# Low weight parts of one expert on GpSimd, one rounding moved, the weight loads written out: a cross-attention and mixture-of-experts kernel on one core

## The chip, the cores and the metric

The kernel runs on one core of one Trainium2 chip. The metric is the device time of one execution in microseconds (us). The engines that matter are TensorE (PE; its weight loads are listed as PEld), VectorE (DVE), ScalarE (ACT), GpSimd (POOL) and SyncE (SP), which issues the large loads and stores. The engines run their own instruction lists in order and meet only at semaphores.

## The reference, cut to what matters

```python
x = x + xattn(ctx, ctx, layernorm(x))            # a long convolution per head, 32 heads
h = layernorm(x)                                 # 2048 tokens of 512
scores = softmax(h @ gate_w.T)                   # 16 experts, the best 4 of each token
...
xg  = xpad[buf]                                  # up to 256 tokens gathered per expert
mid = silu(xg @ w_gate[e]) * (xg @ w_up[e])      # 512 -> 352
y  += scatter(mid @ w_down[e] * wbuf[e])         # 352 -> 512
x  = x + y + shared_ffn(h)
```

Every matrix product of the expert part is done in three passes on numbers split in a high part (rounded to fp32r) and a low part (what is left): high by high, high by low, low by high. So each weight block and each gathered row block needs a rounding (the high part, on ScalarE) and a subtraction (the low part, on VectorE) before TensorE can use it. The tokens are 2048 rows of 512 numbers; `CAP` is 256 and there are 16 experts.

## The kernel before, in words

The first part (to about 345 us) works on head groups: convolutions of key and value products on TensorE, products and sums on VectorE, the pair products and low parts on GpSimd, and the router and the shared feed-forward layer of the group before in between. The second part is a pipeline over the 16 experts. The order of each engine is written out by hand in a function `unit(e, k, ...)` per engine; `k` is `e % 2` and picks one of two sets of buffers. What `unit(e)` holds:

- TensorE: `expert_gu(e, k, 0)` and `expert_gu(e, k, 1)` (24 matmuls each; gate and up products of 128 of the 352 columns), `slots(e + 2)` (16 small matmuls that find the rows of expert e + 2), `rows_t(e + 1)` (8 transposes of the gathered rows of the next expert into PSUM), `expert_down(e - 1)` (18 matmuls) and `expert_gu(e, k, 2)`. The first `expert_gu` of an expert waits for all of its high weights (`ew_h`), all of its low weights (`ew_l`), and the high and low rows (`g_h`, `g_l`).
- ScalarE: four `split_w(e + 1, ., c)` (L1105, the high weights of chunk c, 128 x 704), `e_silu` and `e_round` of each of the three middles (L1134, L1140), `round_rows(e + 1)` (L1127, the high rows, two instructions), `split_d(e)` (L1110, L1111) and `weigh(e - 1)`.
- VectorE: `one_hot(e + 2)` (L1763, 128 x 2048 bf16), `low_w(e + 1, ., c)` for c = 0 to 3 (L1786, 128 x 704 each), `e_middle` and `e_low` of each middle (L1802, L1809), `decode(e + 2)` (five small instructions, L1769 to L1780, that give the row numbers for the gather), `low_rows(e + 1)` (L1794, two instructions) and `low_d(e)` (L1815, L1817). The order is one_hot, low_w 0, low_w 1, e_middle 0, low_w 2, e_low 0, decode, e_middle 1, low_rows, low_w 3, e_low 1, low_d.
- GpSimd: `gather(e + 2)` (L1377, two indirect DMAs) once `decode` has signalled `sl_ok`, and `scatter(e - 1)` (L1390). Between them it has nothing to do.
- SyncE: `next_raw(e)` waits until the high and low parts of the weights of expert e are made, loads the weights of expert e + 2 into the same buffer (L488, L489), waits for the high and low down weights of expert e and loads those of e + 2 (L492, L494). It stood in a hardware loop over pairs of experts.

`unit(0)` is special on every engine: there is no expert before it (`before` is False), so `e_middle(-1, 2)`, `e_low(-1, 2)`, `expert_down(-1)` and `weigh(-1)` are missing, and the weights of expert 1, loaded late because their buffer was in use by the shared layer, are split in it.

Of the kernel before, what the change touches and what calls it, by code (L numbers as in the profile page):

```python
# [18 lines left out]
fp32 = mybir.dt.float32  # L19
# [3 lines left out]
ALU = mybir.AluOpType  # L23
# [7 lines left out]
def wait(eng, sem, value):  # L31

    if not (isinstance(value, int) and value <= 0):
        eng.wait_ge(sem, value)


def xattn_moe_kernel(nc, x, ctx, taps, skip, gate_w, w_gate, w_up, w_down, sw_gate, sw_up, sw_down, out):
    B, ROWS, L = x.shape
    H = taps.shape[0]
    HD = ROWS // H  # L40
    E, _, I = w_gate.shape
    IS = sw_gate.shape[1]
    CAP, TOPK, EPS = 256, 4, 1e-5
    T = B * ROWS
    LB = L // P
# [37 lines left out]
    with es:  # L83
        def sem(name):
            return es.enter_context(nc.semaphore(name))
# [7 lines left out]
        def place(name, shape, dt):  # L93
            size = 1
            for n in shape[1:]:
                size *= n
            size = -(-size * (2 if dt == bf16 else 4) // 32) * 32
            t = nc.alloc_sbuf_tensor_at(name, shape, dt, offset=cursor[0])
            cursor[0] += size
            assert cursor[0] <= arena_base + arena_bytes, (name, cursor[0])  # L100
            return t
# [137 lines left out]
        raw_w = [raw_w0, place("raw_w1", [P, LB, 2 * I], fp32)]  # L239
        raw_d = [raw_d0, place("raw_d1", [P, EJ, L], fp32)]  # L240
        ew = [ew0, place("ew1", [P, LB, 2, 2 * I], fp32r)]
# [55 lines left out]
        rt_c = sem("rt_c")  # L297
        rt_go, rt_step, rt_w = sem("rt_go"), sem("rt_step"), sem("rt_w")
        ew_h, ew_l, ed_h, ed_l = sem("ew_h"), sem("ew_l"), sem("ed_h"), sem("ed_l")
        vals_ok = sem("vals_ok")  # L300
        oh_ok, sl_mm, sl_ok, sl_cp = sem("oh_ok"), sem("sl_mm"), sem("sl_ok"), sem("sl_cp")
        chain = sem("chain")
# [62 lines left out]
        def _(sp):  # L365
# [121 lines left out]
            def load_raw_w(e, k):  # L487
                sp.dma_start(raw_w[k][:, :, 0:I], wg_e[e]).then_inc(raw_in[k], 16)  # L488
                sp.dma_start(raw_w[k][:, :, I:2 * I], wu_e[e]).then_inc(raw_in[k], 16)  # L489

            def load_raw_d(e, k):
                sp.dma_start(raw_d[k][:, 0:2, :], w_down[e, 0:2 * P, :].rearrange("(j p) l -> p j l", p=P))\  # L492
                    .then_inc(rawd_in[k], 16)
                sp.dma_start(raw_d[k][0:EK[2], 2, :], w_down[e, 2 * P:I, :]).then_inc(rawd_in[k], 16)  # L494
# [13 lines left out]

            def next_raw(e, k):
                sp.wait_ge(ew_h, LB * (e + 1))  # L510
                sp.wait_ge(ew_l, LB * (e + 1))
                load_raw_w(e + 2, k)
                sp.wait_ge(ed_h, e + 1)
                sp.wait_ge(ed_l, e + 1)
                load_raw_d(e + 2, k)

            with sp.Fori(0, E // 2 - 1) as i:
                for k in range(2):
                    next_raw(2 * i + k, k)
            sp.wait_ge(out_out, 16 * TT * NG)  # L520
            sp.wait_ge(xn_out, 16 * TT * NG)
            sp.wait_ge(added, 16 * HALVES * E)
# [3 lines left out]
        def _(pe):  # L526
# [289 lines left out]
            def expert_gu(e, k, j):  # L816
                m = EK[j]
                if j == 0:
                    pe.wait_ge(ew_h, LB * e + LB)
                    pe.wait_ge(ew_l, LB * e + LB)  # L820
                    pe.wait_ge(g_h, HALVES * e + HALVES)
                    pe.wait_ge(g_l, HALVES * e + HALVES)
                if isinstance(e, int) and e == 0 and j == TT:
                    pe.wait_ge(mid_ok, SJ * (NG - 1) + 4)
                wait(pe, e_mid, EJ * e - EJ + j + 1)
                for u in range(2):
                    for c in range(LB):
                        for a, b in PASSES:
                            col = u * I + j * P
                            last = pe.matmul(egu[j][0:m, u * CAP:(u + 1) * CAP], ew[k][:, c, a, col:col + m],  # L830
                                             xgT[k][:, c, b, :], start=(c == 0 and (a, b) == PASSES[0]),
                                             stop=(c == LB - 1 and (a, b) == PASSES[-1]))
                last.then_inc(e_mm, 1)
# [75 lines left out]
        def _(act):  # L909
# [192 lines left out]
            def split_w(e, k, c):  # L1102
                act.wait_ge(raw_in[k], 32 * ((e - k) // 2) + 32 if isinstance(e, int) else e * 16 + (32 - 16 * k))
                wait(act, e_mm, EJ * e - EJ)
                act.activation(ew[k][:, c, 0, :], raw_w[k][:, c, :], ACT.Copy).then_inc(ew_h, 1)  # L1105

            def split_d(e, k):
                act.wait_ge(rawd_in[k], 32 * ((e - k) // 2) + 32 if isinstance(e, int) else e * 16 + (32 - 16 * k))
                wait(act, e_dn, HALVES * e - HALVES)
                act.activation(ed[k][:, 0:2, 0, :], raw_d[k][:, 0:2, :], ACT.Copy)  # L1110
                act.activation(ed[k][0:EK[2], 2, 0, :], raw_d[k][0:EK[2], 2, :], ACT.Copy).then_inc(ed_h, 1)  # L1111
# [11 lines left out]
            def round_rows(e, k):  # L1123
                for h in range(HALVES):
                    act.wait_ge(g_tr, HALVES * e + h + 1)
                    wait(act, e_mm, EJ * e - EJ)
                    act.activation(xgT[k][:, :, 0, h * P:(h + 1) * P],  # L1127
                                   yb[:, h, :].rearrange("p (c n) -> p c n", c=LB), ACT.Copy).then_inc(g_h, 1)
# [7 lines left out]
            def e_round(e, k, j):  # L1136
                m, s = EK[j], (EJ * k + j) % 2
                act.wait_ge(e_mid, EJ * e + j + 1)
                wait(act, e_dn, HALVES * e - HALVES)
                act.activation(midh[0:m, EJ * k + j, :], mid[0:m, s, :], ACT.Copy).then_inc(e_midh, 1)  # L1140

            def unit(e, k, before):
                if before:
                    e_round(e - 1, 1 - k, 2)
                for c in range(LB):
                    split_w(e + 1, 1 - k, c)
                e_silu(e, k, 0)
                e_round(e, k, 0)
                e_silu(e, k, 1)
                e_round(e, k, 1)  # L1150
                round_rows(e + 1, 1 - k)
                split_d(e, k)
                if before:
                    weigh(e - 1, 1 - k)
                e_silu(e, k, 2)
# [24 lines left out]
            for e in range(1, E - 2):  # L1180
                unit(e, e % 2, True)
            unit(E - 2, 0, True)
            last_unit(E - 1, 1)


        @block.gpsimd
        def _(pool):
# [183 lines left out]
            def gather(e, k):  # L1371
                pool.wait_ge(sl_ok, e + 1)
                wait(pool, g_tr, HALVES * e - HALVES)
                wait(pool, carried[0], e)
                pool.memset(carrier[:, 0:1], 0.0).then_inc(carried[0], 1)  # L1375
                for h in range(HALVES):
                    pool.indirect_dma_start(xg[k][:, h, :], None, xn_dram,  # L1377
                                            bass.IndirectOffsetOnAxis(slot_rows[:, e, h:h + 1], 0),
                                            bounds_check=T - 1, oob_is_err=False).then_inc(rows_in[k], 16)
# [14 lines left out]
            def unit(e, k, before, next2):  # L1394
                if next2:
                    gather(e + 2, k)
                if before:
                    scatter(e - 1, 1 - k)
# [10 lines left out]
            pool.wait_ge(xn_out, 16 * TT * NG)  # L1409
            gather(0, 0)  # L1410
            gather(1, 1)
            unit(0, 0, False, True)
            for e in range(1, E - 2):
                unit(e, e % 2, True, True)
# [6 lines left out]
        def _(dve):  # L1421
# [361 lines left out]
            def low_w(e, k, c):  # L1783
                dve.wait_ge(ew_h, LB * e + c + 1)
                wait(dve, e_mm, EJ * e - EJ)
                dve.tensor_tensor(ew[k][:, c, 1, :], raw_w[k][:, c, :], ew[k][:, c, 0, :].bitcast(fp32),  # L1786
                                  ALU.subtract).then_inc(ew_l, 1)
# [32 lines left out]
            def unit(e, k, before, next2):  # L1820
                if before:
                    e_middle(e - 1, 1 - k, 2)
                if next2:
                    one_hot(e + 2)
                if before:
                    e_low(e - 1, 1 - k, 2)
                low_w(e + 1, 1 - k, 0)
                low_w(e + 1, 1 - k, 1)
                e_middle(e, k, 0)
                low_w(e + 1, 1 - k, 2)  # L1830
                e_low(e, k, 0)
                if next2:
                    decode(e + 2, k)
                e_middle(e, k, 1)
                low_rows(e + 1, 1 - k)
                low_w(e + 1, 1 - k, 3)
                e_low(e, k, 1)
                low_d(e, k)
                if e and 2 * e + 2 < E:
                    values(2 * e + 2, 2 * e + 4)  # L1840
# [80 lines left out]
```

## Time and profile before

| | us |
|---|---|
| time, median of 3 runs (lowest, highest) | 617.8 (617.42, 619.48) |
| the profiled execution's own time | 618.2 |
| its span, first to last instruction | 616.2 |
| PE, busy of the span | 586.8 (95%) |
| DVE, busy | 486.3 (79%) |
| POOL, busy | 389.9 (63%) |
| ACT, busy | 291.5 (47%) |
| mean granted clock of TensorE, share of full speed (1.00 in every slice after 100 us but the last) | 0.989 |
| TensorE idle in the span's rest after 392 us, for other engines | 1.8, in one wait |

How to read it: the profiled execution is one execution, and its span leaves out 2.0 us (618.2 less 616.2) before the first and after the last instruction. From about 392.4 us to 600 us TensorE works without a gap, with a period of 14.03 us for an expert; the experts' part begins for TensorE at 380.65 us with `expert_gu(0, 0, 0)`. Where a row says "<-DVE ew L1786", the instruction's wait ended when that VectorE instruction signalled.

### The profile page before, as it was taken

The numbers are of one execution on the slowest core, as the hardware profiler recorded it, in microseconds if no ns is written. First come the engines' busy times: TensorE is split into PE (matmuls) and PEld (weight loads), VectorE is DVE, ScalarE is ACT, GpSimd is POOL, SyncE is SP. The second block draws the span as 40 slices with busy tenths as digits, with TensorE's granted clock in tenths as the row PEclk, the third lists the DMA queues.
The fourth block names the chain that finished last, engine by engine and source line by source line (L and its number), as shares of the span: only waits on it lengthen the run. The fifth ranks groups of instructions, "written<-read, shape, count | busy, mean of one in ns | idle before, by whom it ended". The sixth has DMA issues, their size and how long they took to land.

```text
span 616.2 us, 13661 instructions
## 1 busy us (share of the span) xinstructions
PE 586.8 (95%) x4387; PEld 550.3 (89%) x4387; DVE 486.3 (79%) x1279; ACT 291.5 (47%) x521; POOL 389.9 (63%) x502
## 2 busy tenths in 40 slices
PE   3969999999999999999999999899999999999993
PEld 3759998999999999989999898899999999999992
DVE  6998787679779779599699879989887888887730
ACT  2525334434434435345262334566655666656731
POOL 6998898878888888789771282178344433334342
PEclk9988999999999999999999999999999999999997
DMA  6475215136325336142240146788878888788443
GB/s 192 181 250 169 74 70 167 49 86 179 82 80 153 81 94 170 43 132 64 82 115 2 51 160 229 236 245 223 233 222 216 228 233 244 234 230 247 128 55 47
DMA packets 60489, 92.01 MB, mean 149 GB/s; under 512 B 4260, under 2 KB 36004, under 8 KB 60440
## 3 DMA queue, kind: packets, MB, share of 16 engines
q1 hardware_dynamic: 53168, 74.53, 39.3%
q0 software_dynamic: 7168, 16.78, 13.1%
q8 instruction: 27, 0.44, 0.3%
q14 instruction: 22, 0.18, 0.1%
q10 hardware_dynamic: 104, 0.08, 0.0%
HBM read 74.29 MB, written 17.08 MB: 148 GB/s over the span
## 4 chain that ended last, share of the span: by engine, by line
PE 79%; DVE 10%; issue 3%; POOL 3%; ACT 2%; DMA 1%; DVEq 1%; POOLq 0%; SPq 0%; ACTq 0%
PE gu L678 18%; PE gu L830 14%; PE yb L558 11%; PE mb L847 10%; PE gu L716 7%; PE yb L830 7%; PE yb L608 4%; PE mb L530 4%; PE yb L530 2%; DVE prod L1494 2%; DVE oT L1512 1%; POOL kv L1233 1%; DVE prod L1496 1%; DVE ew L1786 1%; PE yb L801 1%
## 5 line engine op out<-in xcount | busy, mean ns | idle before, releaser
L678 PE MATMUL gu<-xT,sw 128*128 128x256 f32 (+2 forms) x1104 | 136.3, 281 | 0.0
L678 PEld LDWEIGHTS gu<-xT,sw 128*128 128x128 f32 (+2 forms) x1104 | 131.8, 180 | 0.4 <-issue 0.2
L1233 POOL TENSOR_TENSOR kv<-kT 128x256 f32 (+3 forms) x232 | 106.8, 499 | 0.0
L1250 POOL TENSOR_TENSOR kvl<-kv,kvh 128x1440 fp32r<-128x1440 f32 (+1 forms) x28 | 87.7, 3131 | 25.7 <-ACT kvh L957 25.5
L1494 DVE TENSOR_TENSOR prod<-yb,qT 128x64 f32<-128x64 f32 (+10 forms) x272 | 74.5, 284 | 18.8 <-PE yb L608 13.5
L957 ACT ACTIVATE kvh<-kv 128x1440 fp32r<-128x1440 f32 (+1 forms) x28 | 37.5, 1339 | 76.1 <-POOL kv L1240 36.9
L1512 DVE TENSOR_REDUCE oT<-prod 128x256 f32<-128x2048 f32 x32 | 72.9, 2277 | 0.1
L558 PE MATMUL yb<-kvh,tlast 128*128 128x288 f32 x280 | 66.1, 297 | 0.0
L1496 DVE TENSOR_TENSOR prod<-yb,qT 128x96 f32<-128x96 f32 (+10 forms) x238 | 63.9, 268 | 0.0
L847 PE MATMUL mb<-ed,midh 128*128 128x512 f32 x180 | 57.4, 400 | 0.0
L1786 DVE TENSOR_TENSOR ew<-raw_w,ew 128x704 fp32r<-128x704 f32 x64 | 55.1, 881 | 0.3 <-ACT ew L1105 0.3
L1375 POOL MEMSET carrier<- 128x1 f32 x16 | 2.5, 158 | 80.8 <-DVE slot_rows L1780 80.8
L830 PE MATMUL gu<-xgT,ew 128*128 128x256 f32 x384 | 47.2, 282 | 1.8 <-DVE ew L1786 1.8
L830 PEld LDWEIGHTS gu<-xgT,ew 128*128 128x128 f32 x384 | 46.4, 190 | 2.1 <-issue 2.0
L558 PEld LDWEIGHTS yb<-kvh,tlast 128*128 128x128 f32 x280 | 48.1, 188 | 0.0
L1105 ACT ACTIVATE ew<-raw_w 128x704 fp32r<-128x704 f32 x64 | 45.4, 777 | 4.5 <-DMA raw_w<-in_L_ffn_w_up_dram 4.5
L830 PE MATMUL gu<-xT,ew 128*128 128x256 f32 x384 | 47.0, 282 | 0.0
L830 PEld LDWEIGHTS gu<-xT,ew 128*128 128x128 f32 x384 | 46.3, 190 | 0.1
L1258 POOL TENSOR_TENSOR midl<-mid,midh 128x256 fp32r<-128x256 f32 x36 | 26.3, 737 | 28.6 <-ACT midh L983 28.5
L1140 ACT ACTIVATE midh<-mid 128x256 fp32r<-128x256 f32 (+1 forms) x48 | 20.1, 418 | 49.6 <-DVE mid L1802 49.6
L716 PE MATMUL gu<-sd,midh 128*128 128x512 f32 x140 | 43.5, 392 | 0.0
L1377 POOL DMA_INDIRECT xg<-normalised_tokens,slot_rows x32 | 33.6, 1051 | 15.1 <-issue 15.1
(219 smaller groups left out, 1322.3 us busy)
## 6 DMA issues: line engine op xcount, KB each, us to landing
raw_w<-in_L_ffn_w_gate_dram SPq DMA_DIRECT2D x16, 704.0 KB, 7.8
raw_w<-in_L_ffn_w_up_dram SPq DMA_DIRECT2D x16, 704.0 KB, 9.2
raw_d<-in_L_ffn_w_down_dram SPq DMA_DIRECT2D x16, 512.0 KB, 4.3
tlast<-toeplitz_taps SPq DMA_DIRECT2D x20, 384.0 KB, 3.6
tstep<-tap_steps SPq DMA_DIRECT2D x20, 256.0 KB, 4.1
c_t<-in_ctx_dram SPq DMA_DIRECT2D x16, 256.0 KB, 4.8
x_t<-in_x_dram SPq DMA_DIRECT2D x16, 256.0 KB, 5.0
toep<-toeplitz_taps SPq DMA_DIRECT2D x8, 512.0 KB, 3.8
```

The source lines that it names most:

```text
L558: last = pe.matmul(yb[:, lb, 0:PW], taps_of(a), (kvh, kvl)[b][:, s, m, :], start=(i == 0 and (a, b) == PASSES[0]), stop=(i == len(parts) - ...
L678: last = pe.matmul(bank[0:m, u * GT:(u + 1) * GT], sw[:, c, a, col:col + m], xT[:, c, b, :], start=(c == 0 and (a, b) == PASSES[0]), stop= ...
L716: last = pe.matmul(sums[:, t, :], (midh, midl)[a][:, j, cols], sd[:, j, b, :], start=False, stop=(j == SJ - 2 and (a, b) == PASSES[-1]))
L830: last = pe.matmul(egu[j][0:m, u * CAP:(u + 1) * CAP], ew[k][:, c, a, col:col + m], xgT[k][:, c, b, :], start=(c == 0 and (a, b) == PASSES ...
L847: last = pe.matmul(mb[:, h, :], lhs[0:EK[j], EJ * k + j, h * P:(h + 1) * P], ed[k][0:EK[j], j, b, :], start=(j == 0 and (a, b) == PASSES[0 ...
L1105: act.activation(ew[k][:, c, 0, :], raw_w[k][:, c, :], ACT.Copy).then_inc(ew_h, 1)
L1233: last = pool.tensor_tensor(to[:, :, POFF[d]:POFF[d] + w], src[:, :, 0:w], src[:, :, d * B:HD * B], ALU.mult)
L1250: pool.tensor_tensor(kvl[:, s, 0:nb, :], kv[:, s, 0:nb, :], kvh[:, s, 0:nb, :].bitcast(fp32), ALU.subtract)\
L1494: last = dve.tensor_tensor(prod[:, lo:hi, d * B // 2:HD * B // 2, d, :], pair, first, ALU.mult)
L1496: last = dve.tensor_tensor(prod[:, lo:hi, 0:w // 2, HD - d, :], pair, second, ALU.mult)
L1512: dve.tensor_reduce(oT[:, :, hl * HD * B:(hl + 1) * HD * B].rearrange("p c (a u) -> p c a u", u=2), prod[:].rearrange("p c a i u -> p c a ...
L1786: dve.tensor_tensor(ew[k][:, c, 1, :], raw_w[k][:, c, :], ew[k][:, c, 0, :].bitcast(fp32), ALU.subtract).then_inc(ew_l, 1)
```

## The change

Three edits, all at the start of the expert pipeline or in who signals whom:

1. The low weight parts of expert 1 for chunks 2 and 3 are computed by GpSimd, right after it has issued the gathers of experts 0 and 1, and no longer by VectorE in `unit(0)`. They signal a new semaphore `ew_lp`; the consumers of low weights (TensorE, and SyncE before it loads over them) wait for both from expert 1 on.
2. In ScalarE's `unit(0)` the rounding of the second middle, `e_round(0, 0, 1)`, comes behind `round_rows(1)` in place of ahead of it.
3. SyncE's loop of weight loads is written out, 14 times `next_raw`.

```diff
+        ew_lp = sem("ew_lp")
+        LENT = LB // 2
+
+        def low_weights(eng, e):
+            first = isinstance(e, int) and e == 0
+            eng.wait_ge(ew_l, LB * e + (LB if first else LB - LENT))
+            if not first:
+                eng.wait_ge(ew_lp, LENT)
...
             def next_raw(e, k):
                 sp.wait_ge(ew_h, LB * (e + 1))
-                sp.wait_ge(ew_l, LB * (e + 1))
+                low_weights(sp, e)
                 load_raw_w(e + 2, k)
...
-            with sp.Fori(0, E // 2 - 1) as i:
-                for k in range(2):
-                    next_raw(2 * i + k, k)
+            for e in range(E - 2):
+                next_raw(e, e % 2)
...
                 if j == 0:
                     pe.wait_ge(ew_h, LB * e + LB)
-                    pe.wait_ge(ew_l, LB * e + LB)
+                    low_weights(pe, e)
...
                 e_silu(e, k, 1)
-                e_round(e, k, 1)
+                if before:
+                    e_round(e, k, 1)
                 round_rows(e + 1, 1 - k)
+                if not before:
+                    e_round(e, k, 1)
                 split_d(e, k)
...
             gather(0, 0)
             gather(1, 1)
+            for c in range(LB - LENT, LB):
+                pool.wait_ge(ew_h, LB + c + 1)
+                pool.tensor_tensor(ew[1][:, c, 1, :], raw_w[1][:, c, :], ew[1][:, c, 0, :].bitcast(fp32),
+                                   ALU.subtract).then_inc(ew_lp, 1)
             unit(0, 0, False, True)
...
                 low_w(e + 1, 1 - k, 1)
                 e_middle(e, k, 0)
-                low_w(e + 1, 1 - k, 2)
+                if before:
+                    low_w(e + 1, 1 - k, 2)
                 e_low(e, k, 0)
                 if next2:
                     decode(e + 2, k)
                 e_middle(e, k, 1)
                 low_rows(e + 1, 1 - k)
-                low_w(e + 1, 1 - k, 3)
+                if before:
+                    low_w(e + 1, 1 - k, 3)
                 e_low(e, k, 1)
```

## Rows read from the trace of the kernel before

**Rows 1.** Timeline of TensorE: start, length, line, what, how many, idle before it.

```profile
387.60 3.06 PE L830 MATMUL yb<-xT,ew 128*96 128x256 f32 x24
392.43 5.95 PE L830 MATMUL gu<-xgT,ew 128*128 128x256 f32 x48 [1.78 <-DVE ew L1786]
```

**Rows 2.** The chain that ended last, in order of time: start, length, what.

```profile
403.89 2.84 PE yb L830 x24
406.72 5.71 PE gu L830 x48
```

**Rows 3.** Timeline of VectorE in unit(0): start, length, line, what.

```profile
382.91 2.28 DVE L1763 TENSOR_TENSOR onehot<-iota_c,rank_in 128x2048 bf16<-128x2048 bf16 x1
385.11 1.69 DVE L1786 TENSOR_TENSOR ew<-raw_w,ew 128x704 fp32r<-128x704 f32 x2
386.71 0.41 DVE L1802 TENSOR_TENSOR mid<-sil,gu 128x256 f32<-128x256 f32 x1
387.04 0.89 DVE L1786 TENSOR_TENSOR ew<-raw_w,ew 128x704 fp32r<-128x704 f32 x1
387.84 0.42 DVE L1809 TENSOR_TENSOR midl<-mid,midh 128x256 fp32r<-128x256 f32 x1
...
388.85 0.42 DVE L1802 TENSOR_TENSOR mid<-sil,gu 128x256 f32<-128x256 f32 x1
390.24 1.29 DVE L1794 TENSOR_TENSOR xgT<-yb,xgT 128x512 fp32r<-128x512 f32 x2 [0.97 <-ACT xgT L1127]
391.45 0.88 DVE L1786 TENSOR_TENSOR ew<-raw_w,ew 128x704 fp32r<-128x704 f32 x1
```

**Rows 4.** Timeline of ScalarE in unit(0).

```profile
381.44 2.84 ACT L1105 ACTIVATE ew<-raw_w 128x704 fp32r<-128x704 f32 x4 [1.98 <-DMA raw_w<-in_L_ffn_w_up_dram]
...
387.16 0.42 ACT L1140 ACTIVATE midh<-mid 128x256 fp32r<-128x256 f32 x1 [2.61 <-DVE mid L1802]
387.48 0.36 ACT L1134 ACTIVATE sil<-gu 128x256 f32<-128x256 f32 x1
389.31 0.42 ACT L1140 ACTIVATE midh<-mid 128x256 fp32r<-128x256 f32 x1 [1.46 <-DVE mid L1802]
389.63 1.06 ACT L1127 ACTIVATE xgT<-yb 128x512 fp32r<-128x512 f32 x2
```

**Rows 5.** Line L1273, GpSimd's low parts of shared weights: ns min/median/max, starts.

```profile
L1273 POOL TENSOR_TENSOR sw<-sw_raw,sw x6: 1668/1692/1719, 30.9 to 49.7; 128x704 fp32r<-128x704 f32 x6
```

**Rows 6.** Timeline of both engines, 83.36 to 84.91 us, one instruction a row.

```profile
83.36 0.69 DVE L1440 TENSOR_TENSOR sd<-x,sd 128x512 fp32r<-128x512 f32 x1
83.44 0.93 POOL L1233 TENSOR_TENSOR kv<-kT 128x128 f32<-128x128 f32 x1
83.96 0.95 DVE L1440 TENSOR_TENSOR sd<-x,sd 128x512 fp32r<-128x512 f32 x1
```

**Rows 7.** Groups by shape, 8 to 20 us: a GpSimd 128-wide product, mean ns.

```profile
L1233 POOL TENSOR_TENSOR kv_more<-kT 128x128 f32<-128x128 f32 x1 | 0.5, 451 | 0.0
```

**Rows 8.** Timeline at 362 to 365 us, both engines.

```profile
362.21 2.29 DVE L1763 TENSOR_TENSOR onehot<-iota_c,rank_in 128x2048 bf16<-128x2048 bf16 x1
362.62 2.17 POOL L1365 TENSOR_TENSOR wt<-wrest,V 128x64 f32<-128x64 f32 x1
```

**Rows 9.** Timeline at 200 to 203 us, both engines.

```profile
200.17 3.31 POOL L1250 TENSOR_TENSOR kvl<-kv,kvh 128x1440 fp32r<-128x1440 f32 x1 [0.55 <-ACT kvh L957]
202.75 0.41 DVE L1548 TENSOR_TENSOR mid<-sil,gu 128x256 f32<-128x256 f32 x1
```

**Rows 10.** Timeline of GpSimd: the last indirect DMA of expert 2's gather.

```profile
391.04 1.00 POOL L1377 DMA_INDIRECT xg<-normalised_tokens,slot_rows  x1 [0.30 <-issue]
```

**Rows 11.** Line L1377 as a whole: from issue to landing.

```profile
DMA to landing us min/median/max: 3.3/3.6/5.4
```

**Rows 12.** Waits of SyncE's queue, 380 to 600 us: total us, times, longest.

```profile
SPq L514 <- DVE ed L1817: 150.7, 14, 11.8
```

**Rows 13.** Timeline of TensorE's weight loads at 603 us.

```profile
603.45 0.30 PEld L858 LDWEIGHTS mb<-ed,midh 96*128 96x128 f32 x2 [0.24 <-issue]
```

## The prediction

> **What bounds the kernel now.** I read the page first. Its busy shares name TensorE (586.8 of 616.2 us), and its chain of waits ends in the experts' part almost wholly in TensorE lines. Then I asked where TensorE is idle there. The chain in order of time shows no gap inside the pipeline: the 24 matmuls at 403.89 us take 2.84, and the next group starts at 406.72, where they end [rows 2]. The timeline of TensorE has one hole: `expert_gu(0, 0, 2)` starts at 387.60, and the next group, `expert_gu(1, 1, 0)`, only at 392.43, after 1.78 us of idle that a VectorE instruction of L1786 ended [rows 1]. A stream of 24 such matmuls takes 2.84, so TensorE could have gone on at 387.60 + 2.84 = 390.44, and the whole hole is 392.43 - 390.44 = 1.99 us. Behind it TensorE is full, so whatever moves the start of `expert_gu(1, 1, 0)` moves the end of the kernel by the same amount, and nothing else in this change can move it by more than that hole on the good side.
>
> The timeline of VectorE then tells what fills the time up to 392.43 [rows 3]: one_hot from 382.91, low_w 0 and 1 of expert 1 from 385.11, the first middle at 386.71, low_w 2 at 387.04, e_low at 387.84, decode, the second middle at 388.85, 0.97 idle, low_rows from 390.24, low_w 3 from 391.45 to 392.33. The idle 0.97 is ScalarE's: it rounds the second middle at 389.31 and only then the rows at 389.63 [rows 4].
>
> **What the change takes out, if nothing gets in its way.** Three terms, each read between starts in [rows 3]:
> - low_w 2 goes. From the start of the first middle to that of e_low it was 387.84 - 386.71 = 1.13. Now e_low waits for ScalarE's rounding, which starts 0.04 behind the middle's end and takes 0.42 [rows 4]: 0.41 + 0.04 + 0.42 and 0.04 to signal are 0.91. Gain 0.22.
> - The rows are rounded ahead of the second middle, so low_rows can follow that middle at once: 390.24 - 388.85 = 1.39 becomes 0.33, the spacing of such a middle (387.04 - 386.71). Gain 1.06.
> - low_w 3 goes: 392.33 less the end of low_rows at 391.53. Gain 0.80.
>
> These are 2.08 us, and low_rows would end at 391.53 - 1.28 = 390.25. With 0.10 us to signal (392.33 to 392.43) TensorE could start at 390.35, before it has finished its own work at 390.44. So undisturbed the hole is gone, and the gain is 1.99.
>
> **What it adds.** Two subtractions of 128 x 704 on GpSimd. The same form on the same engine is on record at L1273, where nothing disturbs it: 1.69 us [rows 5]. They can start when ScalarE has made the high parts of chunks 2 and 3: four in 2.84 us from 381.44, so chunk 2 at about 383.6 and chunk 3 at 384.3 [rows 4]; GpSimd has issued its two gathers by then. Alone they would be over at 387.0, three microseconds ahead of need.
>
> But they are not alone. VectorE and GpSimd hold each other up in this trace whenever both read two operands from SBUF. At 83.36 VectorE starts a subtraction of that kind (0.69). GpSimd's 128-wide product, issued at 83.44, takes 0.93 [rows 6] where 0.45 is its length undisturbed [rows 7]: it ends at 84.37, 0.32 after VectorE's end. VectorE's next subtraction, issued at 83.96, takes 0.95 in place of 0.69 and ends at 84.91, 0.54 behind GpSimd's. So they take turns, one whole instruction each, also where VectorE has its next one ready, and a handed-over turn costs the instruction's own length less 0.13 (GpSimd, 0.45 - 0.32) or 0.15 (VectorE, 0.69 - 0.54). One_hot holds GpSimd up too: a 64-wide GpSimd instruction issued at 362.62 under a one_hot that ran to 364.50 took 2.17 and ended at 364.79 [rows 8]. A VectorE instruction that reads PSUM, such as a middle, isn't held up: 0.41 in the midst of a GpSimd subtraction of 3.31 [rows 9].
>
> Now the order of VectorE in unit(0) has one_hot, low_w 0 and low_w 1 back to back, all three with both operands in SBUF, exactly where GpSimd becomes ready. Step by step:
> - GpSimd's chunk 2 is issued at 383.65 under one_hot, which ends at 385.19 [rows 3]. It gets the turn: 385.19 + 1.69 - 0.13 = 386.75.
> - VectorE's low_w 0, issued at 385.11, waits for it: 386.75 + 0.88 - 0.15 = 387.48.
> - GpSimd's chunk 3 had queued up behind low_w 0: 387.48 + 1.56 = 389.04.
> - low_w 1 waits for that: 389.04 + 0.73 = 389.77.
> - The first middle starts 0.08 before that end, at 389.69. It was 386.71, so it is 2.98 late.
>
> All that follows on VectorE up to low_rows shifts with it. The sum for the start of `expert_gu(1, 1, 0)`: + 2.98 - 0.22 - 1.06 - 0.80 = + 0.90 us. Checked forward: middle 389.69, e_low 390.60, second middle 1.01 later (388.85 - 387.84) at 391.61, low_rows 391.94 to 393.23, TensorE 393.33, against 392.43. ScalarE is in time for it: round 390.14 to 390.56, the silu that follows to 390.84, the rows in 1.06 to 391.9, just ahead of low_rows.
>
> The Trainium skill, in SBUF — State Buffer (section "Who interferes with whom"), gives the reason in general terms: a VectorE instruction with two SBUF inputs takes its second one through the read port that GpSimd uses, and whichever comes second blocks fully. By that rule the sum is the + 0.90 above; without it the sum would be the gain of 1.99. The trace agrees with it by the 2.17 and the 0.95.
>
> **What follows behind it.** The gather of expert 2 waits for `decode`, which is 2.76 late (391.61 for 388.85): its last indirect DMA starts at 391.04 + 2.76 = 393.80 [rows 10] and, with the longest landing on record, 5.4 [rows 11], has landed by 399.2. TensorE asks for those rows 6.11 after the start of `expert_gu(1, 1, 0)` with 48 matmuls and the slots (5.71 + 0.40), so at 399.4. That is covered, by 2.0 at the median landing of 3.6. One_hot of expert 3 and e_low of the third middle come 1.4 later (low_d then waits for ScalarE's split of the down weights, which the moved rounding puts behind the rows) and are still over before TensorE reaches them. VectorE has slack in each unit (79% busy), so the rest catches up. SyncE's loads of expert 3 wait for low_d, as they always do (14 waits, the longest 11.8) [rows 12], about 1.4 later than before; the weights are needed a whole unit after.
>
> **The small edits.** The written-out loop takes two register moves out of an iteration of a queue that is idle for 150 us [rows 12]: 0, with a rival below. The second wait of TensorE, once for each of 15 experts, stands behind four others that cost no gap today [rows 2]: 0 from below; the one place where TensorE's queue takes time for waits in sight is 0.24 us at 603.45 [rows 13], an upper end of 15 x 0.24 = 3.6. I take 0, the row nearest to it being the very place.
>
> **The sum.** The profiled execution took 618.2 us; + 0.9 is 619.1. It lay 0.4 above the median of the runs, 617.8, so the median after should be 618.7.
>
> **Rivals.**
> - *No hold-up* (the two engines don't disturb each other in these instructions): the hole closes, - 1.99, so 615.8. For it speaks only that a VectorE instruction with one operand in PSUM runs undisturbed [rows 9], which these are not; against it [rows 6, 8].
> - *VectorE keeps its turn* while it has instructions ready. Then one_hot and both low_w run as before to 386.80, GpSimd's chunk 2 comes under the first middle (386.80 + 1.56 = 388.36), e_low ends at 388.36 + 0.27 = 388.63, chunk 3 at 390.19, and the small instruction of `decode` that reads two SBUF operands waits for that. The second middle starts at about 390.5, low_rows ends at 392.1, TensorE starts at 392.2: - 0.2, so 617.6. Against it: VectorE's two subtractions at 83.36 and 83.96 let one of GpSimd in between [rows 6].
> - *TensorE's added wait shows* (slower): at each of the 15 places where the wait for `ew_lp` stands, the weight loads start late because the queue has one more instruction to work off than the running matmuls cover. From 0.07 a place on (0.07 x 15 = 1.05, with 0.9 past 0.3%) it decides; at the 0.24 of [rows 13] it is 3.6 + 0.9 = 4.5, so 622.3. Against it: four waits cost nothing there now.
> - *The written-out loads come late* in steady state, by fetches of instructions that a loop doesn't need. It would take over 3 us a load before ScalarE waits; then every expert is late. I give it almost nothing.
>
> **How the numbers follow.** The turn-taking case 0.60; VectorE keeps its turn 0.12; no hold-up 0.13; the added wait 0.07; anything else, such as a gather that lands late, 0.08. A difference of 0.3% (1.85 us, that is 615.95 or 619.65) is about what can be told from no change here. The first case has its own range of 617.9 to 619.9: a turn may cost 0.2 more or less, and the median of three runs moves by half a microsecond (the three lie 2.06 apart). Of it 0.10 lies past 619.65. No hold-up lies at 615.8, just past the lower bound; I count all of it as faster, with 0.03 of the rest. So faster 0.16, slower 0.10 + 0.07 + 0.03 = 0.20, the same 0.64. The range runs from 615.7, which takes in the closed hole, to 620.5, which leaves out most of the added wait.
>
> **What would show it.** Right: in unit(0) GpSimd's first subtraction takes about 3.1 us (383.65 to 386.75) and the second about 2.3; low_w 0 takes 2.4 and low_w 1 2.3 in place of 0.88; TensorE's hole before `expert_gu(1, 1, 0)` is 2.7 in place of 1.78, ended by low_rows (L1794), not by L1786; behind it the period stays 14.03. Wrong: low_w at 0.88 and GpSimd's at 1.69 would mean no hold-up; a hole under 1.78 with both GpSimd instructions behind low_w 1 would mean the other order; gaps of a tenth at the start of every expert would be the added wait.

## The result and the profile after

The changed kernel took 620.69 us (median of 9 runs, 619.22 to 622.04), the kernel before 617.99 (9 runs, 617.42 to 619.56): ratio 1.0035, 95% interval 1.0026 to 1.0044. It is slower by about 2.2 us by the ratio and 2.7 by the medians. The forecast was 618.7, 0.9 slower, in a range of 615.7 to 620.5; the median lies 0.2 past that range, while 2.2 on top of the 617.8 that the forecast started from is 620.0, within it. Line numbers of the changed kernel are higher: VectorE's low_w is L1800, low_rows L1808, GpSimd's new line L1424, `expert_gu` L837.

The timeline of TensorE, changed kernel (start, length, what, idle before it), answers to [rows 1]:

```profile
387.95 3.06 PE L837 MATMUL yb<-xT,ew 128*96 128x256 f32 x24
393.83 7.45 PE L837 MATMUL gu<-xgT,ew 128*128 128x256 f32 x48 [2.83 <-DVE xgT L1808]
```

Two things are to be seen. The hole (the idle time of TensorE ahead of these 48 matmuls) is 2.83 us in place of 1.78, and low_rows ends it. And the 48 matmuls behind it take 7.45 in place of 5.95. The timelines of VectorE and GpSimd, each instruction by itself, answer to [rows 3]:

```profile
383.25 2.28 DVE L1777 TENSOR_TENSOR onehot<-iota_c,rank_in 128x2048 bf16<-128x2048 bf16 x1
383.85 3.23 POOL L1424 TENSOR_TENSOR ew<-raw_w,ew 128x704 fp32r<-128x704 f32 x1 [1.13 <-ACT ew L1112]
385.44 2.38 DVE L1800 TENSOR_TENSOR ew<-raw_w,ew 128x704 fp32r<-128x704 f32 x1
387.04 2.34 POOL L1424 TENSOR_TENSOR ew<-raw_w,ew 128x704 fp32r<-128x704 f32 x1
387.75 2.38 DVE L1800 TENSOR_TENSOR ew<-raw_w,ew 128x704 fp32r<-128x704 f32 x1
390.06 0.41 DVE L1816 TENSOR_TENSOR mid<-sil,gu 128x256 f32<-128x256 f32 x1
392.30 1.28 DVE L1808 TENSOR_TENSOR xgT<-yb,xgT 128x512 fp32r<-128x512 f32 x2
```

GpSimd waits for the end of one_hot, VectorE for GpSimd, GpSimd for VectorE, VectorE for GpSimd: one instruction each. 3.23, 2.38, 2.34, 2.38 where 3.1, 2.4, 2.3, 2.3 were forecast. The busy time by stage shows the rest. Each row has the stage and its length, the busy time of PE, PEld, DVE, ACT and POOL with counts, then the granted clock of TensorE as a share of full speed, the DMA share and GB/s. Changed kernel:

```profile
393.83:401.28 7.45, 7.45 (x54) 7.40 (x55) 7.03 (x10) 4.44 (x9) 1.03 (x2) 0.77 0.76 223
409.63:423.66 14.03, 14.03 (x116) 13.19 (x116) 12.41 (x26) 8.66 (x16) 5.57 (x7) 1.00 0.89 233
...
394.00:395.00 1.00, 1.00 (x6) 1.00 (x6) 0.67 (x1) 0.56 (x2) 0.83 (x1) 0.51 0.44 90
395.00:396.00 1.00, 1.00 (x7) 1.00 (x6) 1.00 (x2) 0.00 (x0) 0.16 (x1) 0.50 0.68 201
397.00:398.00 1.00, 1.00 (x8) 1.00 (x8) 1.00 (x1) 1.00 (x2) 0.00 (x0) 0.78 0.62 86
398.00:399.00 1.00, 1.00 (x11) 1.00 (x10) 1.00 (x3) 1.00 (x3) 0.00 (x0) 1.00 0.91 305
```

The same stretch before:

```profile
392.43:398.38 5.95, 5.95 (x54) 5.90 (x55) 5.95 (x8) 3.41 (x6) 0.00 (x0) 1.00 0.61 182
```

Behind the hole the granted clock is 0.50 (1.2 of 2.4 GHz) from 394.0 to 397.4 us, then full again; later experts keep their 14.03. The difference of the two profiled executions, 616.2 to 618.9, adds up so: `expert_gu(0, 0, 0)` starts 0.32 later (380.97 for 380.65; this comes from ahead of the change, where one wait of TensorE near 8 us took 4.75 for 3.73); from `expert_gu(0, 0, 2)` to `expert_gu(1, 1, 0)` it is 5.88 for 4.83, so 1.05 more; the matmuls at half clock 1.50 more; the rest gives back 0.17.

### The profile page after: what moved, and what is told of

Its sections match the earlier page's. It is cut to its first block, busy times and chain, and to the rows that moved or that the text cites. A ratio compares the mean times of both kernels' runs of the same rounds, so it can differ in the third digit from the quotient of the medians.

```text
span 618.9 us, 13563 instructions
## 1 busy us (share of the span) xinstructions
PE 587.3 (95%) x4387; PEld 550.9 (89%) x4387; DVE 487.3 (79%) x1277; ACT 291.4 (47%) x521; POOL 383.4 (62%) x504
## 4 chain that ended last, share of the span: by engine, by line
PE 79%; DVE 10%; issue 3%; POOL 3%; ACT 2%; DMA 1%; DVEq 1%; POOLq 0%; SPq 0%; ACTq 0%
PE gu L685 18%; PE gu L837 14%; PE yb L565 11%; PE mb L854 10%; PE gu L723 7%; PE yb L837 6%; PE yb L615 4%; PE mb L537 4%; PE yb L537 2%; DVE prod L1508 2%; DVE oT L1526 1%; POOL kv L1243 1%; DVE prod L1510 1%; DVE ew L1800 1%; PE yb L808 1%
## 5 line engine op out<-in xcount | busy, mean ns | idle before, releaser
L1800 DVE TENSOR_TENSOR ew<-raw_w,ew 128x704 fp32r<-128x704 f32 x62 | 56.5, 931 | 0.3 <-ACT ew L1112 0.3
L837 PE MATMUL gu<-xgT,ew 128*128 128x256 f32 x384 | 48.7, 287 | 2.8 <-DVE xgT L1808 2.8
L837 PEld LDWEIGHTS gu<-xgT,ew 128*128 128x128 f32 x384 | 47.9, 195 | 3.1 <-issue 3.0
L837 PE MATMUL gu<-xT,ew 128*128 128x256 f32 x384 | 47.0, 282 | 0.0
L837 PEld LDWEIGHTS gu<-xT,ew 128*128 128x128 f32 x384 | 46.4, 190 | 0.1
```

## The experiments

Ratios are to the kernel before, run beside each group on the same chip: its median was 618.32 for `e1` to `e4`, 617.63 for `e5` to `e8` and 618.38 for `e9`.

**Who holds VectorE up: GpSimd's reads.** `e1_no_read`

```diff
-                pool.tensor_tensor(ew[1][:, c, 1, :], raw_w[1][:, c, :], ew[1][:, c, 0, :].bitcast(fp32),
-                                   ALU.subtract).then_inc(ew_lp, 1)
+                pool.memset(ew[1][:, c, 1, :].bitcast(fp32), 0.0).then_inc(ew_lp, 1)
```

> The changed kernel, in which GpSimd fills the two low chunks of expert 1 with zeros (it writes the same places and signals the same, but reads nothing from SBUF; the low parts of these two chunks are left out of the products). Taking turns over reads of SBUF (my theory): low_w 0 and 1 of VectorE are back at 0.88 each (1.69 for both, where the changed kernel has 4.69), the hole of TensorE ahead of expert 1 closes (under 0.2 us idle, where the changed kernel has 2.83), no clock is lost, and the time is 2.0 below before, 0.9968 of it. If GpSimd's writes, or its work as such, hold VectorE up (rival): low_w keeps over 2 us each and the hole stays over 1.5. If the written-out loads or the added waits cost (rival): the hole closes, but the time stays within 0.5 of before or above it.

Ratio 0.9963 (0.9950 to 0.9977), 616.03 us. TensorE waits for no engine there, the 48 matmuls start at 390.70 with 5.93. VectorE and GpSimd side by side:

```profile
383.10 2.28 DVE L1776 TENSOR_TENSOR onehot<-iota_c,rank_in 128x2048 bf16<-128x2048 bf16 x1
385.30 1.69 DVE L1799 TENSOR_TENSOR ew<-raw_w,ew 128x704 fp32r<-128x704 f32 x2
383.80 1.37 POOL L1424 MEMSET ew<- 128x704 f32 x2 [1.23 <-ACT ew L1112]
```

GpSimd's two writes (383.80 to 385.17) lie wholly under one_hot, which keeps its 2.28. So writing the same places costs nothing; it is the instructions that read that take turns. The same run has the written-out loads and the added waits in it, and they don't keep it from its gain.

**The moved rounding alone.** `e2_round_only`: the kernel before with the change's second edit.

> The kernel before with the second edit alone: the second middle of expert 0 is rounded behind the rows of expert 1. By the terms of the prediction low_rows comes 1.06 earlier, low_w 3 still follows it, the hole shrinks from 1.78 to about 0.7, and the time is 1.06 below before: ratio 0.9983. Rival, that the rounding was covered by something else that is late (the rows from PE, or the silu ahead of it): the hole stays at 1.5 or more and the ratio at 1.000.

Ratio 0.9982 (0.9971 to 0.9992), 616.69 us, the hole 0.70. The term of 1.06 is right: 1.78 - 0.70 = 1.08. **The changed kernel without it**, `e5_no_move`:

> The changed kernel without its second edit: the second middle of expert 0 is rounded ahead of the rows again. By the turns and the term of 1.06 for the rounding, low_rows comes 1.06 later than in the changed kernel, TensorE's idle time is 2.83 + 1.06 = 3.9 us, the clock is at half speed behind it in all executions (48 matmuls in 7.4), and the time is 0.90 + 1.06 + 1.5 = 3.5 above before: ratio 1.0055. If the taking of turns already hides the rounding (rival, since ScalarE is idle longer there): the idle time stays at 2.8 and the ratio at that of the changed kernel, 1.0035.

Ratio 1.0062 (1.0044 to 1.0079), 622.22 us; the idle time is 3.88, 1.05 more than in the changed kernel:

```profile
393.73 1.29 DVE L1805 TENSOR_TENSOR xgT<-yb,xgT 128x512 fp32r<-128x512 f32 x2 [0.97 <-ACT xgT L1134]
395.27 6.91 PE L837 MATMUL gu<-xgT,ew 128*128 128x256 f32 x44 [3.88 <-DVE xgT L1805]
```

These are VectorE's low_rows and TensorE's group behind the hole (this view ends at 402 us; all 48 matmuls take 7.39); the 0.97 for ScalarE is back. So the second edit shortens the idle time by about 1.05 us with and without the first. With the written-out loads near nothing (`e6` below), the loss comes from the first.

**Whether the idle time lowers the clock.** `e3_hole_one`, and `e4_hole_two` with `range(2)`: the kernel before with extra VectorE work that lengthens the hole, GpSimd not involved.

```diff
                 low_rows(e + 1, 1 - k)
+                if not before:
+                    for i in range(1):
+                        dve.tensor_tensor(ew[1][:, 3, 1, :], raw_w[1][:, 3, :], ew[1][:, 3, 0, :].bitcast(fp32),
+                                          ALU.subtract).then_inc(again, 1)
+                        dve.wait_ge(again, i + 1)
                 low_w(e + 1, 1 - k, 3)
```

> The kernel before with one more subtraction of 128x704 on VectorE ahead of low_w 3 in unit(0), GpSimd not involved: the hole of TensorE grows from 1.78 by about 0.95 to 2.7 us, near the 2.83 of the changed kernel. If the length of TensorE's idle time is what makes the granted clock fall (theory): some or all executions show the clock at 0.5 for about 3 us after the hole, the 48 matmuls take 7.4 in place of 5.95, and the time is 0.95 + 0 to 1.5 above before (ratio 1.0015 to 1.004). If the clock fell for another reason that goes with the change, such as GpSimd and VectorE at work together (rival): 48 matmuls stay at 5.95 and the time is 0.95 above before (1.0015).

> As the one before, with two more subtractions: the hole grows by about 1.9 to 3.7 us. Theory (the idle time makes the clock fall): the clock is at 0.5 for some us behind the hole in all executions, 48 matmuls at 7.4 or more, time 1.9 + 1.5 = 3.4 above before, ratio 1.0055. Rival (another reason): 5.95, time 1.9 above before, ratio 1.003.

With two, ratio 1.0055 (1.0042 to 1.0068), 621.61 us. The hole is 3.31, less than the 3.7 expected. The group behind it:

```profile
394.58 7.29 PE L831 MATMUL gu<-xgT,ew 128*128 128x256 f32 x48 [3.31 <-DVE ew L1787]
```

One microsecond of that group by stage, with its clock of 0.50:

```profile
395.00:396.00 1.00, 1.00 (x6) 1.00 (x6) 1.00 (x2) 0.00 (x0) 0.00 (x0) 0.50 0.00 0
```

The clock falls to 0.50 as in the changed kernel, with nothing of the change in the code. With one, ratio 1.0033 (1.0021 to 1.0045), but the profiled execution shows a hole of 2.71 with the clock full and 5.94 for the 48 matmuls; the other seven executions had spans of 617.4 to 618.9 for its 616.3. The longer hole as profiled is worth 0.93 us, a ratio of 1.0015, which lies below that interval, so most of the others lost more than that. Where they lost it their times don't tell; second profiles of this kernel and of the changed one were to show it:

> The kernel with VectorE's one more subtraction, once more: a second profile. Seven of its eight executions had a span of 617.4 to 618.9, the profiled one 616.3 at full clock behind a hole of 2.71. If the fall of the clock is a matter of chance for a hole of this length (theory), a second profile may show 0.5 for some us behind a hole of the same 2.7, with 48 matmuls in about 7.4. If the others were longer for another reason (rival), the clock is full here too and the extra time lies elsewhere.

> The changed kernel once more: a second profile. The turns are the same to 0.05 us (low_w 0 and 1 in 4.69, GpSimd's two in 5.5, idle 2.8), whatever the clock does behind the hole: 0.5 for about 3 us, 48 matmuls in 7.4 and a span of 618 to 619, or full, 5.95 and a span of 616.4 to 617.4.

`e10_hole_one_again` again showed 2.66 idle, a full clock and a span of 616.3, so what the seven had stays unseen. The changed kernel again (`e11_changed_again`, span 618.7) had 2.73 idle and 7.45 for the matmuls:

```profile
393.24:400.69 7.45, 7.45 (x54) 7.40 (x55) 7.03 (x10) 4.44 (x9) 1.03 (x2) 0.77 0.69 210
```

So in the experts' part the clock held behind 1.75, 1.78, 2.66 and 2.71 us of idle time and fell behind 2.73, 2.83, 3.31 and 3.88 (and 5.8, in `e8` below). The fall doesn't come with TensorE's restart: by stages cut finer it came 0.5 and 0.2 us behind the restart in the two profiles of the changed kernel (393.76 for 393.24, 394.02 for 393.83), and 0.4 and 0.2 ahead of it, with TensorE still idle, in `e4` (394.14 for 394.58) and `e5` (395.08 for 395.27). So 2.7 us isn't shown to be a fixed limit, and no profile shows both outcomes of one kernel; what decides near it stays open. The spread of the spans (one of eight at 616.3 here; two of nine at 616.4 and 617.1 in the changed kernel) fits a fall in some executions and not in others, but proves little: the kernel before, with its hole of 1.78, has spans from 614.9 to 617.6 of its own.

The kernel before has such a pause too, far ahead of the experts. TensorE's timeline, then by stage the first 2.95 us of the pause and the 5.85 us of work behind it, in the kernel before:

```profile
43.73 1.09 PE L530 MATMUL mb<-ident,oT 128*128 128x128 f32 x4 [3.94 <-DVE oT L1512]
```

```profile
39.80:42.75 2.95, 0.00 (x0) 0.00 (x0) 2.92 (x11) 0.78 (x2) 2.95 (x3) 1.00 1.02 266
43.73:49.58 5.85, 5.85 (x25) 5.85 (x26) 3.09 (x10) 2.61 (x4) 4.64 (x5) 0.50 0.36 136
```

Behind 3.94 us of idle time TensorE worked 5.85 us at half clock. So the trace of before already held a sign that a pause can cost more than its length.

**The written-out loads alone.** `e6_written_out`

> The kernel before with the third edit alone, SyncE's loads written out 14 times. Theory: the queue waits for low_d anyway, period of an expert 14.03, ratio 1.000. Rival, late loads by fetches of instructions: ScalarE's split of weights waits for DMA in some expert and the period grows; over 1.001.

Ratio 1.0008 (0.9999 to 1.0018), 618.14 us: no difference that can be told, and the profile shows none, with a span of 615.5 and a hole of 1.75. The interval leaves room for up to 1 us.

**A version meant to beat both.** `e7_chunk_wait`: all low parts on VectorE, the rounding moved, and TensorE waits for the last chunk only where it uses it.

```diff
                 if j == 0:
-                    pe.wait_ge(ew_l, LB * e + LB)
+                    pe.wait_ge(ew_l, LB * e + LB - (1 if e == 1 else 0))
...
                     for c in range(LB):
+                        if e == 1 and j == 0 and u == 0 and c == LB - 1:
+                            pe.wait_ge(ew_l, LB * e + LB)
```

> A version meant to beat both: all on VectorE as before, the second edit (the rounding moved), and TensorE waits for the low part of expert 1's chunk 3 only ahead of the first matmul that needs it, the 10th of the group, 9 x 0.119 = 1.07 us in. low_rows ends at 390.47 in the times of the kernel before, so TensorE starts at 390.57, 1.86 earlier than 392.43; low_w 3 is done at 391.3, ahead of 391.64. Idle under 0.2, no clock lost, ratio 0.9970. If the wait in the middle of the group stops the weight loads that run ahead (rival): a gap of some tenths at the 10th matmul, ratio 0.9975 to 0.998.

Ratio 0.9975 (0.9966 to 0.9985), 616.24 us, faster than both kernels. Most of it is the moved rounding, which alone gave 0.9982 (0.9971 to 0.9992) in `e2`; the intervals overlap, so what the later wait adds is shown by the profiles and not by the times: from `expert_gu(0, 0, 2)` to `expert_gu(1, 1, 0)` it is 3.14 us here (390.37 - 387.23) and 3.76 there. TensorE and VectorE's low_rows in its timeline:

```profile
387.23 3.06 PE L832 MATMUL yb<-xT,ew 128*96 128x256 f32 x24
388.83 1.28 DVE L1799 TENSOR_TENSOR xgT<-yb,xgT 128x512 fp32r<-128x512 f32 x2
390.37 5.95 PE L832 MATMUL gu<-xgT,ew 128*128 128x256 f32 x48
```

The wait in the middle of the group costs nothing (5.95 for the 48 matmuls, as before). The start misses the ideal 387.23 + 2.84 = 390.07 by 0.30: it comes 0.26 after low_rows ends at 390.11. I had put 0.10 on that signal.

**GpSimd beside an instruction that reads PSUM.** `e8_one_beside`: the changed kernel with `LENT = 1`, low_w 2 back on VectorE, and

```diff
                 pool.wait_ge(ew_h, LB + c + 1)
+                pool.wait_ge(e_mid, 2)
                 pool.tensor_tensor(...)
```

> The changed kernel, in which GpSimd does chunk 3 alone, and only once the second middle is there, so that it runs beside VectorE's low_rows, which read PSUM; VectorE keeps low_w 2. Theory (only instructions with both operands in SBUF take turns with it): GpSimd's subtraction takes 1.69, low_rows keep 1.28 for both, e_low behind them waits for GpSimd (0.5 more), and TensorE starts when GpSimd is done, 389.27 + 0.05 + 1.69 + 0.1 = 391.1 in the times of before, 1.3 earlier: ratio 0.998. Rival (any VectorE instruction is held up by a GpSimd one): low_rows end only with GpSimd's, at 391.1 + 1.2 = 392.3, TensorE at 392.4, ratio 1.000.

Ratio 1.0106 (1.0091 to 1.0121), 623.99 us: a miss, though the point in question came out as the theory had it.

```profile
388.56 1.28 DVE L1809 TENSOR_TENSOR xgT<-yb,xgT 128x512 fp32r<-128x512 f32 x2
389.76 1.03 DVE L1824 TENSOR_TENSOR midl<-mid,midh 128x256 fp32r<-128x256 f32 x1
392.79 2.28 DVE L1778 TENSOR_TENSOR onehot<-iota_c,rank_in 128x2048 bf16<-128x2048 bf16 x1
388.79 1.71 POOL L1425 TENSOR_TENSOR ew<-raw_w,ew 128x704 fp32r<-128x704 f32 x1 [7.03 <-DVE mid L1817]
392.00 5.08 POOL L1387 DMA_INDIRECT xg<-normalised_tokens,slot_rows  x1 [0.30 <-issue]
```

VectorE first, then GpSimd: GpSimd's 1.71 and low_rows' 1.28 lie side by side undisturbed; e_low, with both operands in SBUF, waits (1.03 for 0.42). TensorE resumed at 390.70. But the gather of expert 2, now behind GpSimd's subtraction, met one_hot, and its second DMA kept GpSimd for 5.08 us in place of 1.00. The waits of TensorE, and its stage behind that wait:

```profile
PE yb L537 <- DMA xg<-normalised_tokens,slot_rows: 5.8, 1, 5.8
```

```profile
402.82:406.24 3.42, 3.42 (x12) 3.09 (x13) 1.47 (x3) 2.01 (x3) 0.00 (x0) 0.50 0.27 78
```

So the loss is the 5.8 us of waiting and, behind it, 3.4 us of work at half clock, less the 1.2 gained at the hole (3.61 for 4.83 from group to group).

**What held the gather.** `e9_late_hot`: the same with

```diff
+                if isinstance(e, int) and e == 1:
+                    dve.tensor_reduce(carrier_d[:, 0:1], ew[1][:, 0, 0, :].bitcast(fp32), AX.X, ALU.max)
                 if next2:
                     one_hot(e + 2)
```

> The kernel with GpSimd's one chunk beside low_rows, and in VectorE's unit(1) a reduction of 128x704 with one operand in SBUF (about 0.8 us, its result unused) ahead of one_hot of expert 3, so that one_hot and what follows it start after the second indirect DMA of expert 2's gather has been worked off by GpSimd. In the kernel without it that DMA took 5.08 us of GpSimd's time (392.00 to 397.08), and TensorE waited 5.8 us for the rows. Theory (what holds the indirect DMA is VectorE's row of two-operand instructions, one_hot, e_low, low_w 0 and 1, that it runs into): it takes 1.00 again, the rows are there in time, TensorE's wait of 5.8 is gone, and the time is that of a start 1.3 earlier than before, ratio 0.998 (0.997 to 0.999). Rival (it was held by the loads on the DMA engines, or by being issued close behind GpSimd's own subtraction): it stays over 4 us, ratio above 1.008.

Ratio 0.9993 (0.9982 to 1.0004), 617.74 us. VectorE and GpSimd in its timeline:

```profile
392.84 0.87 DVE L1839 TENSOR_REDUCE carrier_d<-ew 128x1 f32<-128x704 f32 x1
393.64 2.27 DVE L1778 TENSOR_TENSOR onehot<-iota_c,rank_in 128x2048 bf16<-128x2048 bf16 x1
392.05 1.41 POOL L1387 DMA_INDIRECT xg<-normalised_tokens,slot_rows  x1 [0.31 <-issue]
```

With one_hot 0.85 later, and the loads and GpSimd's order as they were, the DMA is over (393.46) before one_hot begins; it takes 1.41 and TensorE's wait falls from 5.8 to 0.9. So what held it in `e8` was the row of two-operand instructions that one_hot begins, and not the loads or GpSimd's own subtraction. Why it is 1.41 and not 1.00 isn't shown. Not every such row holds a DMA: in `e2` the gather's second DMA (390.38) ran beside low_w 3, e_low and low_d, all with both operands in SBUF, and took 1.10; and in the kernel before one_hot began 0.73 us into the scatter of 434.87, which took 1.58, as the later ones do. What makes the difference stays open. The ratio is 0.001 higher than I expected, about as much as that wait of 0.9: the gather as a whole is still later than in the kernel before.

## Why the prediction was right, and where it fell short

- *What bounds the kernel and where the change can act*: right. Only the one hole moved, the period stayed 14.03.
- *Taking turns*: right, to 0.13 us an instruction, and borne out by `e1`, where writes to the same places without the reads disturb nothing, and by `e8`, where a read beside an instruction on PSUM disturbs nothing. The rivals without a hold-up and with VectorE keeping its turn are out by the rows of L1800 and L1424. The first middle came 6.81 after one_hot's start (390.06 - 383.25), 6.78 were forecast (389.69 - 382.91).
- *The sum at the hole*, + 0.90: measured + 1.05. The term that was off is the signal from low_rows to TensorE, 0.10 taken from the row where low_w ended the hole; it is 0.25 behind low_rows (392.30 + 1.28 = 393.58, TensorE at 393.83; 0.25 again in `e5`, 0.26 in `e7`). Why it is longer there wasn't tried.
- *What a longer hole costs beside itself*: missed. The prediction counted TensorE's pause as its length. The step "whatever moves the start of `expert_gu(1, 1, 0)` moves the end of the kernel by the same amount" failed: behind the 2.83 us of idle time the clock was at half for 3.4 us and the 48 matmuls took 1.50 us more, which is more than the 1.05 by which the hole grew. The two together are 2.55 in the profiled executions and 2.2 by the ratio, where 0.9 was forecast; 1.0035 is just past the bound of 0.3% for "same", and its interval takes the bound in. That the time by the ratio still lies in the range is luck: the upper end was drawn against the added wait, not against the clock. The hole of 1.78 gave no sign of it, but the pause of 3.94 us at 39.8 us in the same trace, with half clock behind it, did, and I didn't look there.
- *The moved rounding*, 1.06: right (1.08 in `e2`, 1.05 in `e5`). *The written-out loads and the added wait*, 0: nothing in the profiles speaks against it, 1.0008 with an interval that takes in 1.
- *The gather behind it*: right in that TensorE didn't wait for it, but the reserve of 2.0 us was less sure than it looked. By `e8` a gather that one_hot begins beside can take 4 us more; in the changed kernel it missed one_hot by luck of 1.2 us (second DMA 394.17 to 395.16, one_hot at 396.40).

## What to carry to other kernels

Before sharing work out to GpSimd, look at what VectorE runs at that time. Here, where both read their operands from SBUF, the two took turns whole instructions at a time, and GpSimd's were the longer ones (1.69 us undisturbed for VectorE's 0.88); beside VectorE instructions that read PSUM, or with GpSimd only writing, neither was slowed. Look first for a wait that is stronger than needed: here a rounding moved behind another and a wait put before the matmul that uses the data took 1.5 us off, most of it the rounding, where the two subtractions on GpSimd, with that same rounding moved, made it 2.2 longer. And price a longer pause of TensorE also with the matmuls behind it at half clock: search the trace for its other pauses and read the clock behind them.

## What was not expected of the hardware

A 2.83 us pause of TensorE was followed by 3.4 us at a granted clock of 0.50, a pause of 2.73 too, one of 2.71 was not. In `e8` an indirect DMA that GpSimd was working off as VectorE began one_hot and the two-operand instructions behind it took 5.08 in place of 1.00 us. The kernel before has two such (scatters of 6.93 and 7.11 us at 407.71 and 421.64, beside one_hot at 407.51 and 421.60), which nobody waits for; in the changed kernel, whose scatters of 409.46 and 423.48 start 0.96 and 1.03 ahead of one_hot, they take 1.57 and 1.59.
